# The last stage's quantizer hands three passes to ScalarE and its transposes wait one tile, and V is prepared two tiles to a bank

## The chip, the cores and the metric

One Trainium2 chip; the kernel runs on all eight of its cores. The metric is the device time of the slowest core, in microseconds. Each core has TensorE (PE, matmuls and their weight loads), VectorE (DVE), ScalarE (ACT), GpSimd (POOL, here only for issuing DMAs) and SyncE (SP, the same). No core waits for another.

## The reference

One transformer layer on x of shape (4, 4096, 1024): a layer norm, an attention over 8 heads of 256 whose keys and values come from a latent of 64, and, beside it on the same normed x, a feed-forward of width 2816 whose inputs and weights are quantized to FP4 and back.

```
xn = layernorm(x)
q = xn @ Wq.T;  kv = xn @ Wkv_down.T;  k = kv @ Wk_up.T;  v = kv @ Wv_up.T
attn = softmax(q k^T / 16) v @ Wo.T            # 8 heads
fq(t): per block of 16: scale = max(max|t| / 6, 1e-12); |t| / scale to the
       grid 0, .5, 1, 1.5, 2, 3, 4, 6; times sign(t) * scale
h = silu(fq(xn) @ fq(w_gate).T) * (fq(xn) @ fq(w_up).T)
out = x + attn + fq(h) @ fq(w_down).T
```

## The kernel before

Core c has half of one batch: 2048 tokens of its own, and the 4096 tokens of the batch as keys. Every engine's instruction list is written out by hand: `eb.em(engine, ...)` appends an instruction to that engine's queue, and `eb.wait(engine, sem, v)` appends a wait until a semaphore has reached v. An engine works its queue in order. Five stages follow one another with barriers between them.

1. Layer norm and quantization of x by DVE, transposes by PE (L340 to L393).
2. The latent and the queries (L435 to L483), and the bounds that take the place of a running maximum in the softmax.
3. Attention, head by head (L589 to L788). A head begins with its preparation. `emit_prep` makes the keys (indices 0 to 15, matmul L618, each 128x512 into one of four PSUM banks `PR4` = psA, psB, psE, psF in turn) and the values (indices 16 to 47, matmul L627, each 128 tokens x 256 into half of a bank). Results with an even index leave PSUM through ACT (L621, L630), those with an odd one through DVE (L623, L631). The values are made in eight groups of four. After each group ACT squares a part of the keys (L654, twice), PE sums the squares (L662) and DVE takes a maximum (L672, L676 or L678). PE's queue has the group's four value matmuls, then L662 twice, then the next group's. Then come the scores (L729), Exp (L743) and the product with V (L759) of four query blocks of 512. After each query block DVE has four units of weight quantization in its queue (`emit_wq_units`), each of which runs the quantizer over 128x512.
4. Softmax denominators and the output projection (L831 to L885).
5. The feed-forward (L927 to L1053). For each of two halves of the width (`ig`) the weights are loaded transposed (L934, L938, L942), and for each half of the tokens (`half`, 1024 each) there is a pass over eight tiles `tt` of 128 tokens. I call it a half pass; there are four. A tile has three chunks of 512, 512 and 384 columns: eight gate matmuls L958 into psD0 and eight up matmuls L962 into psD1, then Silu on ACT (L974) into `gs_c` and the product on DVE (L978) into `h_t`. Both banks are single, so the next chunk's matmuls wait for that product (`hbld`). Then the quantizer takes all 1408 columns of `h_t`, and its last instruction L238 writes `hq_t`. Eleven transposes in f32 (L994, three groups into psA and psB in turn) and three copies on ACT (L1005) bring it to `hqT_b` in bf16. After the eighth tile come the down-projections L1029, 176 matmuls, each of whose 16 results DVE adds to the residual (L1042).

The order in the queues of stage 5 is that of the code: PE has the transposes of a tile right behind its matmuls, ahead of the next tile's; DVE has three products and then the quantizer.

`emit_quant` is one routine for weights, x and h. With `F` columns, in order: L204 block maxima; L205 |t| into pA; L206 and L210 the sign (2 or 0, then 1 or -1) into pK; L208 and L212 the scale and its reciprocal, for F/16 blocks; L214 sign times scale; L217 |t| over scale; L219 to L230 the seven comparisons with the grid; L233 their sum; and L238 the result. The semaphore `lad` counts them, and `wt` waits for one of them.

Of the kernel before, what the change touches and what calls it, by code (L numbers as in the profile page):

```python
# [6 lines left out]
F32 = mybir.dt.float32  # L7
# [75 lines left out]
def build_program(debug=False, stop_after=9):  # L83
# [46 lines left out]
    S = {}  # L130
    for s in ["x_in", "lnv", "lna", "lnd", "lnap", "xq", "tr", "trev",
# [3 lines left out]
              "ffh", "sil", "hbld", "hq", "fftr", "fftrev", "ffdn", "ssq", "srw", "wkl", "lad"]:  # L135
# [45 lines left out]
    def emit_quant(eb, F, src, dst, PL):  # L181
# [3 lines left out]
        L = S['lad']  # L185

# [402 lines left out]
    for h in range(NH):  # L589
# [17 lines left out]
        def emit_prep(rng):  # L607
            for idx in rng:
# [38 lines left out]
        for grp in range(8):  # L647
            emit_prep(range(16 + 4 * grp, 16 + 4 * grp + 4))
# [264 lines left out]
    hq_t = sb("hq_t", [128, 1408], F32, es_b5)  # L913
# [12 lines left out]
    ftr_glob = 0  # L926
    for ig in range(2):  # L927
# [19 lines left out]
        for half in range(2):  # L947
            toff = half * 1024
            eb.wait('scalar', S['avq'], S['avq'].n)
            for tt in range(8):  # L950
                for ci, (c0, clen) in enumerate(NCH):
# [19 lines left out]
                    if S['hbld'].n > 0:  # L971
# [15 lines left out]
                for b_ in range(3):
                    js = [4, 4, 3][b_]
                    pbk = SBK[ftr_glob % 2]
                    if ftr_glob >= 2:  # L990
                        eb.wait('tensor', S['fftrev'], ftr_glob - 1)
                    for j in range(js):
                        c = b_ * 4 + j
                        ins = (lambda e, c=c, j=j, pbk=pbk: e.transpose(  # L994
                            pbk[:, j * 128:(j + 1) * 128], hq_t[:, c * 128:(c + 1) * 128], ident_t[:]))
                        if j == js - 1:
                            S['fftr'].n += 1
                            eb.em('tensor', lambda e, ins=ins: ins(e).then_inc(S['fftr'].h, 1))
                        else:
                            eb.em('tensor', ins)  # L1000
                    eb.wait('scalar', S['fftr'], S['fftr'].n)
                    S['fftrev'].n += 1
                    dst = hqT_b[:, b_ * 4:b_ * 4 + js, tt * 128:(tt + 1) * 128]
                    src = pbk[:, 0:js * 128].rearrange("p (c n) -> p c n", c=js)
# [97 lines left out]
```

## Time and profile before

| | us |
|---|---|
| median of 3 runs (4534.31 to 4548.57) | 4536.94 |
| the profiled execution, device time | 4542.34 |
| its span, first to last instruction of the slowest core | 4540.5 |
| spans of the eight cores | 4522.9 to 4540.5 |
| busy in the span: PE, DVE, ACT | 2552.1, 2607.8, 1116.9 |

The engines' busy times are sums over stages with different limits; the stages themselves are told apart by cutting the span into stretches. Times below are in microseconds from the span's start unless marked ns. The last stage's matmuls begin at 3008. The profile also gives the granted clock of TensorE: 1.00 is its level of 2.4 GHz, 0.50 that of 1.2 GHz.

### The profile page before, as it was taken

The page shows a single profiled execution, that of the slowest core. Times are in us where ns is not written, and L with a number is a line of the kernel's source. Part 1 is how long each engine was busy: PE and PEld are TensorE (multiplying, and loading weights), DVE is VectorE, ACT ScalarE, POOL GpSimd, SP SyncE. Part 2 cuts the span into 40 slices and gives each one's busy share as a digit, 9 for nine tenths or more (in the row PEclk, how much of TensorE's full clock was granted, in tenths as well). Part 3 has the DMA queues.
Part 4 walks back from the last instruction along what each step waited for, and adds up shares of the span by engine and source line. Part 5 has one row for each costly group of instructions (what it writes and reads, how often), then busy time and mean ns, then how long its engine had stood idle before and what let it go on. Part 6 is the DMA issues. An engine that isn't in the chain of part 4 may idle for free. (4 is left out here: it accounts for less than half of the span.)

```text
span 4540.5 us, 36505 instructions; the slowest of 8 cores (4522.9 to 4540.5 us)
## 1 busy us (share of the span) xinstructions
PE 2552.1 (56%) x9848; PEld 950.3 (21%) x9848; DVE 2607.8 (57%) x4169; ACT 1116.9 (25%) x1835; POOL 105.7 (2%) x199
## 2 busy tenths in 40 slices
PE   1113193197878787878888786823353352335335
PEld 1112040022222222222222222411121121112112
DVE  7888604757585857575757524125645542564554
ACT  1112030154545454545444450000000000000000
POOL 0000000000000000000000000000000000000000
PEclk9999995598888888898989795966787676668777
DMA  1112210001010101010101002350020015002002
GB/s 47 29 36 79 48 19 0 29 22 35 22 35 21 37 17 40 18 35 19 34 16 33 18 10 56 141 111 0 0 74 0 0 64 87 0 0 74 0 0 65
DMA packets 126530, 156.30 MB, mean 34 GB/s; under 512 B 77824, under 2 KB 88320, under 8 KB 124288
## 3 DMA queue, kind: packets, MB, share of 16 engines
q1 hardware_dynamic: 110368, 127.56, 10.1%
q0 software_dynamic: 15968, 26.42, 2.4%
q8 instruction: 89, 1.46, 0.1%
q14 instruction: 105, 0.86, 0.1%
HBM read 98.89 MB, written 46.66 MB: 32 GB/s over the span
## 5 line engine op out<-in xcount | busy, mean ns | idle before, releaser
L743 ACT ACTIVATE pbuf<-psA,negB_col 128x512 bf16<-128x512 f32 x512 | 352.1, 688 | 349.5 <-PE psA L729 349.5
L978 DVE TENSOR_TENSOR h_t<-gs_c,psD 128x512 f32<-128x512 f32 (+1 forms) x96 | 61.7, 643 | 650.4 <-ACT gs_c L974 650.4
L743 ACT ACTIVATE pbuf<-psB,negB_col 128x512 bf16<-128x512 f32 x512 | 351.4, 686 | 287.6 <-PE psB L729 286.9
L958 PE MATMUL psD<-wgq_b,xqT_sb 128*128 128x512 bf16 (+1 forms) x768 | 209.6, 426 | 232.5 <-DMA wdq_b<-WdqN 124.3
L204 DVE TENSOR_REDUCE pbm<-wbuf 128x32 f32<-128x512 f32 (+1 forms) x136 | 91.2, 670 | 401.1 <-DMA WdqN<-wqout 163.5
L759 PE MATMUL psC<-pbuf,V_h 128*128 128x512 bf16 x1024 | 310.9, 386 | 18.5 <-ACT pbuf L743 18.5
L759 PE MATMUL psD<-pbuf,V_h 128*128 128x512 bf16 x1024 | 304.5, 379 | 27.5 <-ACT pbuf L743 27.5
L729 PE MATMUL psA<-qT_all,kT_h 128*128 128x512 bf16 x1024 | 316.6, 392 | 0.4 <-DVEq L701 0.4
L729 PE MATMUL psB<-qT_all,kT_h 128*128 128x512 bf16 x1024 | 313.6, 388 | 0.0
L994 PE MATMUL psB<-ident_t,hq_t 128*128 128x128 f32 x176 | 48.3, 426 | 375.3 <-DVE hq_t L238 375.0
L994 PE MATMUL psA<-ident_t,hq_t 128*128 128x128 f32 x176 | 48.3, 425 | 375.2 <-DVE hq_t L238 375.2
L974 ACT ACTIVATE gs_c<-psD 128x512 f32<-128x512 f32 (+1 forms) x96 | 53.9, 562 | 656.8 <-PE psD L962 656.8
L759 PE MATMUL psE<-pbuf,V_h 128*1 128x512 bf16 x512 | 195.7, 382 | 0.0
L759 PE MATMUL psF<-pbuf,V_h 128*1 128x512 bf16 x512 | 193.0, 377 | 0.0
L962 PE MATMUL psD<-wuq_b,xqT_sb 128*128 128x512 bf16 (+1 forms) x768 | 168.6, 363 | 0.0
L1029 PE MATMUL psC<-hqT_b,wdq_b 128*128 128x512 bf16 x704 | 164.0, 397 | 4.9 <-ACT hqT_b L1005 3.3
L958 PEld LDWEIGHTS psD<-wgq_b,xqT_sb 128*128 128x128 bf16 x768 | 82.1, 112 | 349.7 <-issue 309.6
L326 PE MATMUL psA<-ident_t,xq_f 128*128 128x128 f32 x64 | 17.4, 427 | 232.5 <-DVE xq_f L238 232.5
L759 PEld LDWEIGHTS psC<-pbuf,V_h 128*128 128x128 bf16 x1024 | 98.4, 98 | 150.4 <-issue 39.7
L759 PEld LDWEIGHTS psD<-pbuf,V_h 128*128 128x128 bf16 x1024 | 97.6, 98 | 153.6 <-issue 40.8
L1042 DVE TENSOR_TENSOR obuf<-rbuf,psC 128x512 f32<-128x512 f32 x64 | 43.8, 688 | 140.8 <-PE psC L1029 118.4
L1005 ACT CAST hqT_b<-psB 128x512 bf16<-128x512 f32 (+1 forms) x48 | 26.4, 550 | 392.5 <-PE psB L994 392.5
(197 smaller groups left out, 4426.6 us busy)
## 6 DMA issues: line engine op xcount, KB each, us to landing
xbuf<-x_tok SPq DMA_DIRECT2D x16, 1024.0 KB, 6.0
rbuf<-resid_scr SPq DMA_DIRECT2D x32, 512.0 KB, 5.3
wbuf<-Wg SPq DMA_DIRECT2D x44, 256.0 KB, 2.8
wbuf<-Wu SPq DMA_DIRECT2D x44, 256.0 KB, 2.8
wbuf<-Wd SPq DMA_DIRECT2D x40, 256.0 KB, 2.7
xt_buf<-xT_own SPq DMA_DIRECT2D x8, 1024.0 KB, 6.8
resid_scr<-rstage SPq DMA_DIRECT2D x8, 1024.0 KB, 4.7
resid_scr<-obuf SPq DMA_DIRECT2D x16, 512.0 KB, 2.9
```

The lines of the kernel that those rows point to most:

```text
L204: t_bm = op(lambda e: e.tensor_reduce(out=pbm[:, 0:NB], in_=src3, axis=AX.X, op=ALU.max, apply_absolute_value=True))
L729: ins = (lambda e, h=h, qq=qq, kc=kc, m=m, pb=pb: e.matmul(pb[:, :], kT_h[:, m, kc * 128:(kc + 1) * 128], qT_all[:, 2 * h + m, qq * 512:(q ...
L743: eb.em('scalar', lambda e, cglob=cglob, pb=pb: e.activation(out=pbuf[:, cglob % 2, :], in_=pb[:, :], func=AF.Exp, bias=negB_col[:], scale ...
L759: ins = (lambda e, kc=kc, cg=cg, lo=lo, hi=hi, dstp=dstp, dsl=dsl: e.matmul(dstp[dsl, 0:512], V_h[:, kc, lo:hi], pbuf[:, cg % 2, :], start ...
L958: eb.em('tensor', lambda e, tt=tt, c0=c0, clen=clen, kc2=kc2, pg=pg, toff=toff: e.matmul(pg[:, 0:clen], xqT_sb[:, kc2, toff + tt * 128:tof ...
L962: ins = (lambda e, tt=tt, c0=c0, clen=clen, kc2=kc2, py=py, toff=toff: e.matmul(py[:, 0:clen], xqT_sb[:, kc2, toff + tt * 128:toff + (tt + ...
L974: eb.em('scalar', lambda e, clen=clen, pg=pg: e.activation(out=gs_c[:, 0:clen], in_=pg[:, 0:clen], func=AF.Silu).then_inc(S['sil'].h, 1))
L978: eb.em('vector', lambda e, c0=c0, clen=clen, py=py: e.tensor_tensor(out=h_t[:, c0:c0 + clen], in0=gs_c[:, 0:clen], in1=py[:, 0:clen], op= ...
L994: ins = (lambda e, c=c, j=j, pbk=pbk: e.transpose(pbk[:, j * 128:(j + 1) * 128], hq_t[:, c * 128:(c + 1) * 128], ident_t[:]))
L1005: eb.em('scalar', lambda e, dst=dst, src=src: e.copy(dst, src).then_inc(S['fftrev'].h, 1))
L1029: ins = (lambda e, m=m, n2=n2, it=it, pb=pb: e.matmul(pb[:, :], wdq_b[:, it, m * 128:(m + 1) * 128], hqT_b[:, it, n2 * 512:(n2 + 1) * 512] ...
L1042: eb.em('vector', lambda e, m=m, n2=n2, pb=pb: e.tensor_tensor(out=obuf[:, m % 2, n2 * 512:(n2 + 1) * 512], in0=rbuf[:, m % 2, n2 * 512:(n ...
```

## The change

It has three parts.

1. `emit_quant` gets an option `act_abs`, used in stage 5 alone. With it, ACT writes |t| into pA (Abs) and the sign into pK (Sign) and counts them in a new semaphore `aab`; L205, L206 and L210 are left out on DVE. ACT waits first for the quantizer of the tile before (`hq`) and for this tile's products (`hbld`). DVE waits for Sign ahead of L214 and for Abs ahead of L217. At the start of each tile DVE waits for `aab`.
2. `hq_t` has two buffers. The transposes of a tile and their copies are no longer put into the queues behind its quantizer, but behind the next tile's; those of the last tile of a half pass are put right behind.
3. In the preparation of a head the 32 value matmuls are taken in pairs. Two write the two halves of one bank, and one instruction of 128x512 takes both out. A group has two such pairs in place of four single matmuls: the first pair's bank is emptied by ACT, the second's by DVE.

The diff, cut to its core:

```
@@ -178,11 +178,19 @@
     SBK = [psA, psB]
     OAB = [(psC0, psC1, psE), (psD0, psD1, psF)]
 
-    def emit_quant(eb, F, src, dst, PL):
+    def emit_quant(eb, F, src, dst, PL, act_abs=False):
         NB = F // 16
         pA, pC, pD, pK = PL['pA'], PL['pC'], PL['pD'], PL['pK']
         v = 'vector'
         L = S['lad']
+        if act_abs:
+            AB = S['aab']
+            AB.n += 1
+            eb.em('scalar', lambda e: e.activation(out=pA[:, 0:F], in_=src, func=AF.Abs).then_inc(AB.h, 1))
+            a_abs = AB.n
+            AB.n += 1
+            eb.em('scalar', lambda e: e.activation(out=pK[:, 0:F], in_=src, func=AF.Sign).then_inc(AB.h, 1))
+            a_sg = AB.n
 
         def op(fn, inc=True):
             if inc:
@@ -202,18 +210,26 @@
         sb_ = pscale[:, 0:NB].unsqueeze(2).broadcast_to([128, NB, 16])
         rb = prcp[:, 0:NB].unsqueeze(2).broadcast_to([128, NB, 16])
         t_bm = op(lambda e: e.tensor_reduce(out=pbm[:, 0:NB], in_=src3, axis=AX.X, op=ALU.max, apply_absolute_value=True))
-        t_abs = op(lambda e: e.scalar_tensor_tensor(out=pA[:, 0:F], in0=src, scalar=-1.0, in1=src, op0=ALU.mult, op1=ALU.max))
-        t_sg = op(lambda e: e.tensor_scalar(out=pK[:, 0:F], in0=src, scalar1=0.0, scalar2=2.0, op0=ALU.is_ge, op1=ALU.mult))
+        if not act_abs:
+            t_abs = op(lambda e: e.scalar_tensor_tensor(out=pA[:, 0:F], in0=src, scalar=-1.0, in1=src, op0=ALU.mult, op1=ALU.max))
+            t_sg = op(lambda e: e.tensor_scalar(out=pK[:, 0:F], in0=src, scalar1=0.0, scalar2=2.0, op0=ALU.is_ge, op1=ALU.mult))
         wt(t_bm)
         t_sc = op(lambda e: e.tensor_scalar(out=pscale[:, 0:NB], in0=pbm[:, 0:NB], scalar1=6e-12, scalar2=1.0 / 6.0, op0=ALU.max, op1=ALU.mult))
-        wt(t_sg)
-        t_sg1 = op(lambda e: e.tensor_single_scalar(out=pK[:, 0:F], in_=pK[:, 0:F], scalar=1.0, op=ALU.subtract))
+        if not act_abs:
+            wt(t_sg)
+            t_sg1 = op(lambda e: e.tensor_single_scalar(out=pK[:, 0:F], in_=pK[:, 0:F], scalar=1.0, op=ALU.subtract))
         wt(t_sc)
         t_rcp = op(lambda e: e.reciprocal(prcp[:, 0:NB], pscale[:, 0:NB]))
-        wt(t_sg1)
+        if act_abs:
+            eb.wait(v, S['aab'], a_sg)
+        else:
+            wt(t_sg1)
         t_ss = op(lambda e: e.tensor_tensor(out=K3, in0=K3, in1=sb_, op=ALU.mult))
         wt(t_rcp)
-        wt(t_abs)
+        if act_abs:
+            eb.wait(v, S['aab'], a_abs)
+        else:
+            wt(t_abs)
         t_A = op(lambda e: e.tensor_tensor(out=A3, in0=A3, in1=rb, op=ALU.mult))
         wt(t_A)
         tc = op(lambda e: e.tensor_single_scalar(out=pC[:, 0:F], in_=pA[:, 0:F], scalar=0.25, op=ALU.is_gt))
@@ -615,22 +631,28 @@
                         eb.wait('tensor', S['qpj'], kv_base_d + pidx // 2 + 1)
...
                 else:
-                    mt = idx - 16
-                    ins = (lambda e, h=h, mt=mt, pb=pb: e.matmul(
+                    mt = (idx - 16) * 2
+                    ins2 = [(lambda e, h=h, mt=mt, pb=pb: e.matmul(
                         pb[0:128, 0:256], kvT_b[:, mt * 128:(mt + 1) * 128],
-                        wvuh[:, h % 2, :], start=True, stop=True))
-                    eva = (lambda e, mt=mt, pb=pb: e.copy(V_h[:, mt, 0:256], pb[0:128, 0:256]))
-                    evd = (lambda e, mt=mt, pb=pb: e.tensor_copy(V_h[:, mt, 0:256], pb[0:128, 0:256]))
-                S['prep'].n += 1
-                eb.em('tensor', lambda e, ins=ins: ins(e).then_inc(S['prep'].h, 1))
+                        wvuh[:, h % 2, :], start=True, stop=True)),
+                            (lambda e, h=h, mt=mt, pb=pb: e.matmul(
+                        pb[0:128, 256:512], kvT_b[:, (mt + 1) * 128:(mt + 2) * 128],
+                        wvuh[:, h % 2, :], start=True, stop=True))]
+                    dst = V_h[:, mt:mt + 2, 0:256]
+                    srcp = pb[0:128, 0:512].rearrange("p (c n) -> p c n", c=2)
+                    eva = (lambda e, dst=dst, srcp=srcp: e.copy(dst, srcp))
+                    evd = (lambda e, dst=dst, srcp=srcp: e.tensor_copy(dst, srcp))
+                for k2, ins in enumerate(ins2):
+                    S['prep'].n += 1
+                    eb.em('tensor', lambda e, ins=ins: ins(e).then_inc(S['prep'].h, 1))
                 if idx % 2 == 0:
                     eb.wait('scalar', S['prep'], S['prep'].n)
                     S['kvev'].n += 1
@@ -645,7 +667,7 @@
         eb.wait('scalar', S['qpj'], kv_base_d + 8)
         mmp_tgt = [0] * 8
         for grp in range(8):
-            emit_prep(range(16 + 4 * grp, 16 + 4 * grp + 4))
+            emit_prep(range(16 + 2 * grp, 16 + 2 * grp + 2))
             if grp >= 1:
                 eb.wait('scalar', S['bnd'], mmp_tgt[grp - 1])
             sq_base = S['sco'].n
@@ -910,7 +932,7 @@
     wdq_b = sb("wdq_b", [128, 11, 1024], BF16, es_b5)
     gs_c = sb("gs_c", [128, 512], F32, es_b5)
     h_t = sb("h_t", [128, 1408], F32, es_b5)
-    hq_t = sb("hq_t", [128, 1408], F32, es_b5)
+    hq_t = sb("hq_t", [128, 2, 1408], F32, es_b5)
     hqT_b = sb("hqT_b", [128, 11, 1024], BF16, es_b5)
     rbuf = sb("rbuf", [128, 2, 1024], F32, es_b5)
     obuf = sb("obuf", [128, 2, 1024], F32, es_b5)
@@ -924,6 +946,32 @@
     IG = [0, 1408]
     NCH = [(0, 512), (512, 512), (1024, 384)]
     ftr_glob = 0
+    lgq = 0
+    pend_tr = None
+
+    def emit_tr(eb, lg, tt, hq_tgt):
+        nonlocal ftr_glob
+        eb.wait('tensor', S['hq'], hq_tgt)
+        for b_ in range(3):
+            js = [4, 4, 3][b_]
+            pbk = SBK[ftr_glob % 2]
+            if ftr_glob >= 2:
+                eb.wait('tensor', S['fftrev'], ftr_glob - 1)
+            for j in range(js):
+                c = b_ * 4 + j
+                ins = (lambda e, c=c, j=j, pbk=pbk, lg=lg: e.transpose(
+                    pbk[:, j * 128:(j + 1) * 128], hq_t[:, lg % 2, c * 128:(c + 1) * 128], ident_t[:]))
+                if j == js - 1:
+                    S['fftr'].n += 1
+                    eb.em('tensor', lambda e, ins=ins: ins(e).then_inc(S['fftr'].h, 1))
+                else:
+                    eb.em('tensor', ins)
+            eb.wait('scalar', S['fftr'], S['fftr'].n)
+            S['fftrev'].n += 1
+            dst = hqT_b[:, b_ * 4:b_ * 4 + js, tt * 128:(tt + 1) * 128]
+            src = pbk[:, 0:js * 128].rearrange("p (c n) -> p c n", c=js)
+            eb.em('scalar', lambda e, dst=dst, src=src: e.copy(dst, src).then_inc(S['fftrev'].h, 1))
+            ftr_glob += 1
     for ig in range(2):
         i0 = IG[ig]
         if True:
@@ -948,6 +996,7 @@
             toff = half * 1024
             eb.wait('scalar', S['avq'], S['avq'].n)
             for tt in range(8):
+                eb.wait('vector', S['aab'], S['aab'].n)
                 for ci, (c0, clen) in enumerate(NCH):
                     s_ = half * 24 + tt * 3 + ci
                     pg = psD0
@@ -978,32 +1027,22 @@
                     eb.em('vector', lambda e, c0=c0, clen=clen, py=py: e.tensor_tensor(
                         out=h_t[:, c0:c0 + clen], in0=gs_c[:, 0:clen], in1=py[:, 0:clen],
                         op=ALU.mult).then_inc(S['hbld'].h, 1))
+                lg = lgq
+                eb.wait('scalar', S['hq'], S['hq'].n)
+                eb.wait('scalar', S['hbld'], S['hbld'].n)
                 eb.wait('vector', S['hbld'], S['hbld'].n)
-                eb.wait('vector', S['fftr'], S['fftr'].n)
-                last = emit_quant(eb, 1408, h_t[:, 0:1408], hq_t[:, 0:1408], PL5)
+                if lg >= 2:
+                    eb.wait('vector', S['fftr'], 3 * (lg - 1))
+                last = emit_quant(eb, 1408, h_t[:, 0:1408], hq_t[:, lg % 2, 0:1408], PL5, act_abs=True)
                 S['hq'].n += 1
                 eb.em('vector', lambda e, last=last: last(e).then_inc(S['hq'].h, 1))
-                eb.wait('tensor', S['hq'], S['hq'].n)
...
+                if pend_tr is not None:
+                    pend_tr()
+                pend_tr = (lambda lg=lg, tt=tt, hq_tgt=S['hq'].n: emit_tr(eb, lg, tt, hq_tgt))
+                lgq += 1
+            if pend_tr is not None:
+                pend_tr()
+                pend_tr = None
             if debug and half == 0 and ig == 0:
                 eb.wait('sync', S['fftrev'], S['fftrev'].n)
                 S['out'].n += 16
```

## Rows read from the trace of the kernel before

**Rows 1.** The page's costliest groups: busy, mean ns, idle ahead and its releaser.

```profile
L994 PE MATMUL psB<-ident_t,hq_t 128*128 128x128 f32 x176 | 48.3, 426 | 375.3 <-DVE hq_t L238 375.0
```

**Rows 2.** Engines by stretch: PE, PEld, DVE, ACT, POOL busy, clock; first half pass, sum.

```profile
3008.00:3337.00 329.00, 113.78 (x472) 56.58 (x472) 185.00 (x160) 26.69 (x48) 0.00 (x0) 0.70 0.01 3
...
sum 1307.00, PE 445.75 PEld 223.95 DVE 741.38 ACT 105.88 POOL 0.00; mean PE 111.44 PEld 55.99 DVE 185.34 ACT 26.47 POOL 0.00
```

**Rows 3.** The timeline of one tile in the middle of a half pass.

```profile
3260.23 0.69 DVE L978 TENSOR_TENSOR h_t<-gs_c,psD 128x512 f32<-128x512 f32 x1 [8.91 <-ACT gs_c L974]
...
3261.06 1.89 PE L958 MATMUL psD<-wgq_b,xqT_sb 128*128 128x512 bf16 x8 [1.68 <-DVE h_t L978]
...
3266.36 1.46 PE L958 MATMUL psD<-wgq_b,xqT_sb 128*128 128x384 bf16 x8 [1.69 <-DVE h_t L978]
...
3270.63 1.62 DVE L204 TENSOR_REDUCE pbm<-h_t 128x88 f32<-128x1408 f32 x1 [0.21 <-DVE h_t L978]
...
3274.51 0.20 DVE L208 TENSOR_SCALAR pscale<-pbm 128x88 f32<-128x88 f32 x1
...
3275.50 0.70 DVE L212 RECIPROCAL prcp<-pscale 128x88 f32<-128x88 f32 x1
3276.12 1.56 DVE L214 TENSOR_TENSOR PL5pK<-PL5pK,pscale 128x1408 f32<-128x1408 f32 x1
...
3290.66 1.63 DVE L238 TENSOR_TENSOR hq_t<-PL5pC,PL5pK 128x1408 f32<-128x1408 f32 x1 [0.17 <-DVE PL5pC L233]
```

**Rows 4.** The timeline around the first down-projection and the second half pass.

```profile
3331.62 1.63 DVE L238 TENSOR_TENSOR hq_t<-PL5pC,PL5pK 128x1408 f32<-128x1408 f32 x1 [0.17 <-DVE PL5pC L233]
...
3337.11 40.91 PE L1029 MATMUL psC<-hqT_b,wdq_b 128*128 128x512 bf16 x176 [0.82 <-ACT hqT_b L1005]
...
3377.86 1.89 PE L958 MATMUL psD<-wgq_b,xqT_sb 128*128 128x512 bf16 x8
...
3392.73 1.62 DVE L204 TENSOR_REDUCE pbm<-h_t 128x88 f32<-128x1408 f32 x1 [0.21 <-DVE h_t L978]
```

**Rows 5.** ACT's groups by form, last stage and squares of the keys.

```profile
L654 ACT ACTIVATE sqv_t<-kT_h 128x512 bf16<-128x512 bf16 x128 | 73.7, 627 | 0.0
L974 ACT ACTIVATE gs_c<-psD 128x512 f32<-128x512 f32 x64 | 38.2, 597 | 533.6 <-PE psD L962 533.6
...
L974 ACT ACTIVATE gs_c<-psD 128x384 f32<-128x384 f32 x32 | 15.7, 491 | 123.2 <-PE psD L962 123.2
...
L920 ACT ACT_TABLE_LOAD x1 | 1.3, 1283 | 229.4 <-PEq L892 229.4
```

**Rows 6.** The chain that ended last, at starts of chunk 0.

```profile
3008.41 3.47 PE psD L958 x8
3011.88 1.74 PE psD L962 x8
...
3254.36 3.29 PE psD L958 x8
...
3798.64 3.57 PE psD L958 x8
3802.21 2.46 PE psD L962 x8
```

**Rows 7.** DVE's groups by form, one line of the quantizer.

```profile
L222 DVE SCALAR_TENSOR_TENSOR PL3pC<-PL3pA,PL3pC 128x512 f32<-128x512 f32 x112 | 76.8, 685 | 0.0
...
L222 DVE SCALAR_TENSOR_TENSOR PL2pC<-PL2pA,PL2pC 128x512 f32<-128x512 f32 x8 | 5.5, 686 | 0.0
```

**Rows 8.** The timeline of one group of V's preparation.

```profile
898.65 0.39 PE L627 MATMUL psA<-wvuh,kvT_b 64*128 64x256 bf16 x1
...
898.84 0.42 PE L627 MATMUL psB<-wvuh,kvT_b 64*128 64x256 bf16 x1
...
899.14 0.37 ACT L630 CAST V_h<-psA 128x256 bf16<-128x256 f32 x1 [1.57 <-PE psA L627]
...
899.83 1.15 ACT L654 ACTIVATE sqv_t<-kT_h 128x512 bf16<-128x512 bf16 x2
```

More of the change, by code:

```diff
@@ L134, in build_program @@
               "xt16", "rs", "rr", "out", "fw", "xqr", "kv_pe", "q_pe", "prep", "pbev",
-              "ffh", "sil", "hbld", "hq", "fftr", "fftrev", "ffdn", "ssq", "srw", "wkl", "lad"]:
+              "ffh", "sil", "hbld", "hq", "fftr", "fftrev", "ffdn", "ssq", "srw", "wkl", "lad", "aab"]:
         S[s] = Sem(nc, es_sh, "s_" + s)
@@ L617, in emit_prep @@
                     m, n = idx // 8, idx % 8
-                    ins = (lambda e, h=h, m=m, n=n, pb=pb: e.matmul(
+                    ins2 = [(lambda e, h=h, m=m, n=n, pb=pb: e.matmul(
                         pb[:, :], wkuh[:, h % 2, m * 128:(m + 1) * 128],
-                        kvT_b[:, n * 512:(n + 1) * 512], start=True, stop=True))
+                        kvT_b[:, n * 512:(n + 1) * 512], start=True, stop=True))]
                     eva = (lambda e, m=m, n=n, pb=pb: e.copy(
@@ L980, in build_program @@
                         op=ALU.mult).then_inc(S['hbld'].h, 1))
+                lg = lgq
+                eb.wait('scalar', S['hq'], S['hq'].n)
+                eb.wait('scalar', S['hbld'], S['hbld'].n)
                 eb.wait('vector', S['hbld'], S['hbld'].n)
-                eb.wait('vector', S['fftr'], S['fftr'].n)
-                last = emit_quant(eb, 1408, h_t[:, 0:1408], hq_t[:, 0:1408], PL5)
+                if lg >= 2:
+                    eb.wait('vector', S['fftr'], 3 * (lg - 1))
+                last = emit_quant(eb, 1408, h_t[:, 0:1408], hq_t[:, lg % 2, 0:1408], PL5, act_abs=True)
                 S['hq'].n += 1
                 eb.em('vector', lambda e, last=last: last(e).then_inc(S['hq'].h, 1))
-                eb.wait('tensor', S['hq'], S['hq'].n)
[L987 to L1004, printed above, removed]
-                    eb.em('scalar', lambda e, dst=dst, src=src: e.copy(dst, src).then_inc(S['fftrev'].h, 1))
-                    ftr_glob += 1
+                if pend_tr is not None:
[5 more added lines that the diff above has]
+                pend_tr = None
             if debug and half == 0 and ig == 0:
```

## The prediction

> **What bounds the kernel now.** I read the page's costliest groups first. The transposes of `hq_t` idle 375 us behind the last instruction of the quantizer, twice, once for each bank [rows 1]: in the last stage TensorE waits for VectorE, tile after tile. Then I cut the last stage into stretches. Its four half passes over eight token tiles, from the first gate matmul to the first down-projection matmul, take 1307 us of the 4540.5, and in them PE is busy 446 us and DVE 741 us, with a granted clock of 0.70 [rows 2]. Neither engine is full: they take turns. The timeline of one tile says how [rows 3]. Chunk 1 starts at 3261.06, chunk 2 at 3266.36, the quantizer's first instruction L204 at 3270.63, and its last, L238, ends at 3290.66 + 1.63 = 3292.29. That is 21.66 us; transposes and chunk 0 of the next tile follow only then, which is PE's idleness of [rows 1]. One tile takes about 1307 / 32 = 40.8 us.
>
> The attention stage has another limit, and the change touches it at one place, the preparation of V, read from the timeline of one group [rows 8].
>
> **Part 1: three DVE passes go to ACT.** L205, L206 and L210 leave the quantizer of the last stage. What is left ahead of L214: L204 (1.62 us), L208 (0.20), L212 (0.70, but it starts 0.62 ahead of L214) [rows 3]. A result that is waited for costs 0.17 more, as ahead of L238 [rows 3]; before, other instructions covered this. So L208 starts 1.62 + 0.17 = 1.79 us after L204, L212 at 1.79 + 0.20 + 0.17 = 2.16, L214 at 2.78, where it started at 3276.12 - 3270.63 = 5.49. The quantizer falls by 2.71 to 18.95 us, if Abs and Sign are ready.
>
> No row has Abs or Sign. ACT took 597 ns for 512 columns and 491 for 384, 0.83 ns a column; 128x512 from SBUF took 627 [rows 5]. For 1408 columns that is 0.627 + 896 x 0.00083 = 1.37 us. Both may start when the last h_t product is done, 0.1 us ahead of L204, as their other wait is for the quantizer before. The second follows 0.1 early as ACT's do, and ends at -0.1 + 1.27 + 1.37 = 2.54, with 0.1 for the wait 2.64: just in time for L214 at 2.78. Bounds: L214 can't come before L204 allows, so the gain is at most 2.71; if ACT ran these at twice my price, L214 would be 2.6 later and the gain would be nothing. I take 2.71, because ACT's rows agree on the rate. The Trainium skill ("ScalarE: Activation LUTs", Rules for kernel authors) speaks against this move: simple elementwise work such as max and mul belongs on VectorE, with up to 3x in bf16. Here the data are f32 and the passes leave the engine that everybody waits for. By the rule the move would gain nothing, and the sum would be that of the rival "ACT is slow" below; no row of this case times the two functions.
>
> **Part 2: transposes one tile late.** `emit_tr` of tile t-1 now stands behind the matmuls of tile t, so in PE's queue the order is chunks 0 to 2 of tile t, transposes of t-1, chunk 0 of t+1. All of the last two can run under quantizer t. Chunk 1 can't: its banks psD0/psD1 are single, so it waits for the product L978 of chunk 0, which DVE does behind quantizer t. So the serial chain of a tile becomes
>
> - quantizer: 18.95
> - from its end to chunk 1: L978 starts 0.1 early (nothing awaited), takes 0.69, and PE follows 0.14 later (3260.23 + 0.69 to 3261.06 [rows 3]): 0.73
> - chunk 1 to chunk 2: 5.30; chunk 2 to L204: 4.27 [rows 3]
>
> Together 29.25 us, at the full clock. But PE now idles between chunk 0 and chunk 1. What lies under the quantizer: transposes, of which the third group must wait for the first group's copy, which on ACT stands behind Abs and Sign (2.5 + 0.6 + 0.1 = 3.2 us after L204), three more transposes with at most 3 x 0.43 = 1.3 [rows 1], and chunk 0 with at most 16 x 0.43 = 6.9, ends by 11.4, with its Silu at about 12. Chunk 1 comes at 18.95 + 0.73 = 19.7. So the cover has 7 to 8 us to spare, and PE pays that idleness with its clock. Rows: after the idle times ahead of the first and third half pass, the first eight matmuls took 3.47 and 3.57 us in place of 1.74, and in the third half pass the next eight took 2.46 [rows 6]: 0.43 us a matmul is the 1.2 GHz level, 0.22 the 2.4 GHz one. The loss is 1.73 and 1.83 + 0.72 = 2.55 us. Before, this loss fell on chunk 0; now on chunk 1. A tile in the middle of a pass lost 3.29 - 1.74 = 1.55 [rows 6], with transposes ahead of its chunk 0. I take 1.7, between the two lower ones, since most tiles are such. A tile then takes 29.25 + 1.7 = 30.95 us; with the bounds 1.55 and 2.55 it is 30.8 to 31.8, and with all 16 matmuls at the low level (3.4) 32.65.
>
> The second `hq_t` buffer serves only this delay: L238 waits for transposes two tiles back, long done. The new wait of DVE for ACT at each tile's head asks for what L214 has already had. Nothing new goes to SP, POOL or a DMA queue in this stage.
>
> **A half pass.** The first tile has nothing to overlap: 3392.73 - 3377.86 = 14.87 us from chunk 0 to L204 [rows 4], plus the clock's 1.73 and 2.55 in the first and third pass. Then seven periods, a last quantizer of 18.95, and from its end to the down-projection 3337.11 - (3331.62 + 1.63) = 3.86 [rows 4], as the last transposes have no cover. All four: 4 x (14.87 + 18.95 + 3.86) + 4.3 + 28 x 30.95 = 150.7 + 4.3 + 866.6 = 1021.6 us. Before 1307: the change is -285 us. The down-projections read and write the same and stay.
>
> **Part 3: V two tiles to a bank.** The 256 V matmuls stay; 256 evictions of 256 columns become 128 of 512, shared as before between ACT and DVE. What sets a group's length is the start of Square L654, for which PE's next matmuls wait; DVE's evictions lie beside it. Before, it starts 899.83 - 898.65 = 1.18 after the first V matmul. After, ACT waits for the second matmul, like the one that ends at 898.84 + 0.42 = +0.61; plus 0.10 it starts the copy, whose 512 columns let Square start 0.60 - 0.10 = 0.50 later [rows 5, 8]: 1.21. That is 0.03 a group, 64 groups, +2 us; I call it nothing. Bounds: the whole of one saved eviction (0.37 x 64 = -24 us), and a second matmul wholly exposed (0.42 x 64 = +27). The price follows the rows closely, so I keep 10 us of them each way.
>
> **Sum.** 4542.3 (profiled execution) - 285 = 4257; against its span, 4540.5 - 285 = 4255. The profiled execution was 5 us above the median of 4536.9, which gives 4536.9 - 285 = 4252 us. Its own range is 4228 to 4285.
>
> **Rivals.**
>
> - *A table load for Sign.* If Sign is not in the table that holds Silu, ACT loads on the way to Sign and back to Silu. A load took 1.28 us [rows 5]; the first delays L214, the second is under the quantizer. 32 x (2.64 + 1.28 - 2.78) = 36 us: 4288. Against it: Square, Exp and copies alternate in the attention stage with no load but the stages' three. The Trainium skill (same page, Table sets: the hidden batching unit) lists copy, identity, relu and abs as in every set, and does not list sign. No run yet shows it. Chance 0.04.
> - *ACT is slow.* At twice my price for Abs and Sign, L214 waits for ACT, 32 x 2.6 = 83 us: 4335. Against it ACT's rate in [rows 5]. Chance 0.03.
> - *The clock stays low.* Chunks 1 and 2 entirely at 1.2 GHz: 3.4 + 2.6 in place of 1.7, 28 x 4.3 = 120 us: 4372. For it: more but shorter idle times. Against it: it rose in each pass while chunk 0 ran [rows 6]. Chance 0.05.
> - *No overlap of chunk 0.* If its Silu came behind something that lasts as long as the quantizer, a tile had some 5.0 + 1.7 us more: 28 x 6.7 = 188 us, 4440. Against it the 7 to 8 us to spare. Chance 0.04.
> - *Slower: contention under the quantizer.* Before, DVE quantized alone; now PE and ACT use the memories meanwhile. If this stretched DVE's instructions, each per cent would cost 32 x 0.19 = 6 us. From 285 / 6 = 47% on, the kernel is slower; at 60% it takes 4252 + 364 = 4616. Against it: the same L222 took 685 ns while attention ran on PE and ACT, and 686 with DVE alone [rows 7]. Chance 0.01.
>
> **How the numbers follow.** Forecast 0.83, rivals 0.17 together. The range of 8 in 10 takes the V part's 10 us and an excess of the clock to 2.55, and reaches to the table load: 4225 to 4292. A measurement of this kernel can tell a change of about 0.3%, 14 us, from none; every case but the last is far beyond it on the faster side. Faster 0.97, same 0.01, slower 0.02 (contention, and something unnamed).
>
> **What would show it.** Right: L205, L206 and L210 absent from the last stage's DVE, L204 to the end of L238 18.95 us, two ACT instructions of 1.37; PE's transposes and a chunk of 16 matmuls under it; chunk 1 with matmuls of 0.43 first; tiles 31 us apart; half passes of 252 to 256 us; Square 1.2 us behind a group's first V matmul, as before. Wrong: ACT_TABLE_LOAD more than three times; DVE's L214 waiting for ACT; chunk 2 at 0.33 us a matmul; L978 waiting for its Silu right behind the quantizer.

## The result, and the profile after

The changed kernel takes 0.9376 of the time of the kernel before, 95% interval 0.9353 to 0.9399. On the 4541 us that the kernel before took in these runs that is 4258 us, 283 us less (273 to 294). The forecast was 4252. The profiled execution took 4249.6 us, its span 4248.0.

Numbers in what follows that combine a run's ratio with a time use the same 4541 us. A few executions in which the cores of one die ran at a lower clock are left out of all ratios. Line numbers moved: L204 is L212 now, L208 L217, L212 L222, L214 L227, L238 L254; the transposes L994 are L962 and their copies L973, the matmuls L958 and L962 are L1007 and L1011, Silu is L1023, the product L1027 and the down-projection L1068.

The last stage first, the four half passes as stretches (busy time of PE, PEld, DVE, ACT, POOL, then the granted clock, as in [rows 2]):

```profile
3006.00:3262.00 256.00, 118.94 (x472) 55.03 (x472) 160.51 (x136) 46.32 (x64) 0.00 (x0) 0.74 0.01 4
...
sum 1028.00, PE 478.85 PEld 220.55 DVE 643.19 ACT 184.83 POOL 0.00; mean PE 119.71 PEld 55.14 DVE 160.80 ACT 46.21 POOL 0.00
```

These stretches are cut at whole microseconds, and the last, from 3950 to 4207, reaches 2.7 us into the down-projection, which starts at 4204.29. From the first gate matmul to the first down-projection matmul the four passes take 256.1, 257.1, 258.0 and 253.7 us, together 1025, where they took 1307. PE has the same matmuls and 30 us more of busy time, as more of them run at the low clock; DVE has 98 us less, which is the three passes that left it; ACT 79 us more. A tile in the middle of the first half pass answers to [rows 3]:

```profile
3177.90 1.38 ACT L189 ACTIVATE PL5pA<-h_t 128x1408 f32<-128x1408 f32 x1 [0.75 <-DVE h_t L1027]
3178.02 1.62 DVE L212 TENSOR_REDUCE pbm<-h_t 128x88 f32<-128x1408 f32 x1 [0.21 <-DVE h_t L1027]
3179.18 1.36 ACT L192 ACTIVATE PL5pK<-h_t 128x1408 f32<-128x1408 f32 x1
...
3180.45 0.56 ACT L973 CAST hqT_b<-psA 128x512 bf16<-128x512 f32 x1
3180.68 1.60 DVE L227 TENSOR_TENSOR PL5pK<-PL5pK,pscale 128x1408 f32<-128x1408 f32 x1
...
3181.83 3.62 PE L1007 MATMUL psD<-wgq_b,xqT_sb 128*128 128x512 bf16 x8
...
3188.24 0.60 ACT L1023 ACTIVATE gs_c<-psD 128x512 f32<-128x512 f32 x1 [5.63 <-PE psD L1011]
...
3195.25 1.63 DVE L254 TENSOR_TENSOR hq_t<-PL5pC,PL5pK 128x1408 f32<-128x1408 f32 x1 [0.17 <-DVE PL5pC L249]
...
3197.62 3.45 PE L1007 MATMUL psD<-wgq_b,xqT_sb 128*128 128x512 bf16 x8 [9.54 <-DVE h_t L1027]
...
3208.76 1.62 DVE L212 TENSOR_REDUCE pbm<-h_t 128x88 f32<-128x1408 f32 x1 [0.21 <-DVE h_t L1027]
```

Count from L212 at 3178.02. Abs starts 0.12 ahead of it, Sign 1.28 later, and Sign ends at 3180.54. L227 needs it and starts at 3180.68, 2.66 after L212, with no idle time of its own: ACT is just in time. The quantizer ends at 3196.88, after 18.86 us. Under it PE has the last transposes, held until ACT's first copy at 3180.45 + 0.56, and chunk 0, whose Silu starts at 3188.24. Then PE idles until 3197.62. Chunk 1 begins there with eight matmuls in 3.45 us, the low clock: TensorE's granted clock had fallen during this idle time, and from 3192 to 3200 it was 0.50. The next tile's quantizer starts at 3208.76: 30.74 us from tile to tile.

The chain that ended last shows how a pass settles (starts and lengths; L1007 x8 is the first half of a chunk, L1011 x8 the second):

```profile
3042.25 3.57 PE psD L1007 x8
3045.82 2.49 PE psD L1011 x8
...
3074.22 3.57 PE psD L1007 x8
...
3105.22 3.57 PE psD L1007 x8
...
3197.62 3.45 PE psD L1007 x8
...
3262.20 39.84 PE psC L1068 x176
...
3336.36 3.57 PE psD L1007 x8
3339.93 2.22 PE psD L1011 x8
3344.10 2.68 PE psD L1007 x8
3346.77 1.78 PE psD L1011 x8
...
4204.29 39.85 PE psC L1068 x176
```

Chunk 1 of the pass's second tile needs 3.57 + 2.49 us where the high clock would give 3.48, a loss of 2.6. The next ones begin 31.97 and 31.00 us later and lose 2.0 and 1.83, until at 3197.62 the loss is 1.7; from there the tiles are 30.73 apart. The other passes settle in the same way, but from other values: the second tile of the second pass (3336.36) loses 2.3 us in chunk 1 and 1.7 more in chunk 2, where the granted clock was low again, and takes 33.3 us in all. PE idled 16.1 us ahead of chunk 1 in that tile, as in the second tile of the first and the third pass, and 9.5 us in the settled tile above. The first down-projection takes 39.84 us where it took 40.91 [rows 4].

ACT's groups, beside [rows 5]:

```profile
L189 ACT ACTIVATE PL5pA<-h_t 128x1408 f32<-128x1408 f32 x32 | 44.1, 1377 | 24.4 <-DVE h_t L1027 24.4
L192 ACT ACTIVATE PL5pK<-h_t 128x1408 f32<-128x1408 f32 x32 | 43.5, 1360 | 0.0
...
L942 ACT ACT_TABLE_LOAD x1 | 1.3, 1283 | 230.6 <-PEq L914 230.6
```

Abs and Sign took 1.38 and 1.36 us. The table load is one of the same three as before, so Abs and Sign run between two Silus without a load of their own.

And one group of V's preparation, beside [rows 8]: two matmuls fill psA, one ACT copy takes both out, and Square follows.

```profile
897.31 0.39 PE L643 MATMUL psA<-wvuh,kvT_b 64*128 64x256 bf16 x1
...
897.50 0.42 PE L646 MATMUL psA<-wvuh,kvT_b 64*128 64x256 bf16 x1
...
898.01 0.59 ACT L651 CAST V_h<-psA 128x512 bf16<-128x512 f32 x1 [1.78 <-PE psA L646]
...
898.49 1.15 ACT L676 ACTIVATE sqv_t<-kT_h 128x512 bf16<-128x512 bf16 x2
```

Square starts 898.49 - 897.31 = 1.18 us after the group's first matmul. Before it was 1.18.

### The profile page after: what moved, and what is told of

It reads as the page before. It is cut to its first block and busy times, and to the rows that moved or that the text cites. A ratio compares the mean times of both kernels' runs of the same rounds, so it can differ in the third digit from the quotient of the medians.

```text
span 4248.0 us, 36150 instructions; the slowest of 8 cores (4236.9 to 4248.0 us)
## 1 busy us (share of the span) xinstructions
PE 2576.2 (61%) x9848; PEld 946.0 (22%) x9848; DVE 2505.2 (59%) x4009; ACT 1185.5 (28%) x1835; POOL 106.1 (2%) x199
## 5 line engine op out<-in xcount | busy, mean ns | idle before, releaser
L1007 PE MATMUL psD<-wgq_b,xqT_sb 128*128 128x512 bf16 (+1 forms) x768 | 251.7, 491 | 502.3 <-DVE h_t L1027 379.6
L1027 DVE TENSOR_TENSOR h_t<-gs_c,psD 128x512 f32<-128x512 f32 (+1 forms) x96 | 61.6, 641 | 458.5 <-ACT gs_c L1023 458.5
L212 DVE TENSOR_REDUCE pbm<-wbuf 128x32 f32<-128x512 f32 (+1 forms) x136 | 91.2, 670 | 400.8 <-DMA WdqN<-wqout 163.0
L1023 ACT ACTIVATE gs_c<-psD 128x512 f32<-128x512 f32 (+1 forms) x96 | 53.9, 562 | 967.4 <-PE psD L1011 967.4
L781 PE MATMUL psC<-pbuf,V_h 128*128 128x512 bf16 x1024 | 311.0, 386 | 17.9 <-ACT pbuf L765 17.8
L1007 PEld LDWEIGHTS psD<-wgq_b,xqT_sb 128*128 128x128 bf16 x768 | 89.2, 122 | 644.1 <-issue 621.7
L1011 PE MATMUL psD<-wuq_b,xqT_sb 128*128 128x512 bf16 (+1 forms) x768 | 186.8, 390 | 0.0
L1068 PE MATMUL psC<-hqT_b,wdq_b 128*128 128x512 bf16 x704 | 159.4, 391 | 3.3 <-ACT hqT_b L973 3.3
L781 PEld LDWEIGHTS psD<-pbuf,V_h 128*128 128x128 bf16 x1024 | 97.5, 97 | 153.6 <-issue 40.8
L342 PE MATMUL psA<-ident_t,xn_scr 128*128 128x128 f32 x128 | 34.8, 427 | 134.4 <-DVE xn_scr L385 134.4
L888 PE MATMUL psC<-o_all,wo_b 128*128 128x512 bf16 x512 | 112.9, 384 | 1.5 <-DVE o_all L870 1.5
L1011 PEld LDWEIGHTS psD<-wuq_b,xqT_sb 128*128 128x128 bf16 x768 | 82.9, 108 | 103.3 <-issue 47.6
```

Of the source, the lines that this page charges most:

```text
L212: t_bm = op(lambda e: e.tensor_reduce(out=pbm[:, 0:NB], in_=src3, axis=AX.X, op=ALU.max, apply_absolute_value=True))
L342: ins = (lambda e, c=c, j=j, pbank=pbank, src_tile=src_tile: e.transpose(pbank[:, j * 128:(j + 1) * 128], src_tile[:, c * 128:(c + 1) * 12 ...
L781: ins = (lambda e, kc=kc, cg=cg, lo=lo, hi=hi, dstp=dstp, dsl=dsl: e.matmul(dstp[dsl, 0:512], V_h[:, kc, lo:hi], pbuf[:, cg % 2, :], start ...
L888: ins = (lambda e, m=m, n=n, kc=kc, pb=pb: e.matmul(pb[:, :], wo_b[:, kc, m * 128:(m + 1) * 128], o_all[:, kc, n * 512:(n + 1) * 512], sta ...
L1007: eb.em('tensor', lambda e, tt=tt, c0=c0, clen=clen, kc2=kc2, pg=pg, toff=toff: e.matmul(pg[:, 0:clen], xqT_sb[:, kc2, toff + tt * 128:tof ...
L1011: ins = (lambda e, tt=tt, c0=c0, clen=clen, kc2=kc2, py=py, toff=toff: e.matmul(py[:, 0:clen], xqT_sb[:, kc2, toff + tt * 128:toff + (tt + ...
```

## The experiments

**The parts one by one.** Each is the kernel before with one part of the change. `e_act` has part 1: the transposes are put behind each quantizer again (`hq_t` keeps its two buffers, which then serve nothing).

```diff
-                if pend_tr is not None:
-                    pend_tr()
-                pend_tr = (lambda lg=lg, tt=tt, hq_tgt=S['hq'].n: emit_tr(...))
+                emit_tr(eb, lg, tt, S['hq'].n)
```

> Part 1 alone: Abs and Sign on ACT, but the transposes right behind each tile's quantizer and V as before. Theory A (costs add): each of 32 quantizers is 2.7 to 2.8 us shorter and the matmuls' loss to the low clock stays at about 1.55 us, so tiles are 38.2 us apart in place of 40.96 and the kernel takes 4541 - 32 x 2.75 = 4453 us. Theory B (the loss depends on how the idle time falls, and settles with the period): the loss moves by up to 1 us a tile, tiles are 37.2 to 39.2 apart and equal once settled, 4425 to 4485 us. Theory C (ACT's copies and waits are what counts, not DVE): no change, 4541.

Ratio 0.9763 (0.9732 to 0.9793), 4433 us. The chain, at the starts of chunk 0:

```profile
3196.92 2.88 PE psD L1001 x8
...
3234.67 2.78 PE psD L1001 x8
...
3272.33 2.72 PE psD L1001 x8
```

Tiles are 37.75 and 37.66 us apart, not 38.2. The quantizer is 18.86 us as in the changed kernel, so DVE's 2.8 us are as priced; but chunk 0 loses only 2.88 - 1.74 = 1.14, then 1.04 and 0.98 us to the low clock, where it lost 1.55 [rows 6]. Theory A has the gain some 20 us too small, theory B holds, theory C falls. Of those 20 us the clock is one part: the 28 tiles of the trace are 86 us shorter in sum, and 28 x 2.8 = 78 of them are the quantizer's.

`e_late` has part 2 alone:

```diff
-                last = emit_quant(eb, 1408, ..., PL5, act_abs=True)
+                last = emit_quant(eb, 1408, ..., PL5)
```

> Part 2 alone: transposes one tile late with two buffers, quantizer all on DVE as before, V as before. Theory A (a fixed loss of 1.7 us to the low clock): the tile takes 21.66 + 0.73 + 5.30 + 4.27 + 1.7 = 33.65 us against 40.96, 28 x 7.3 = 205 us less, 4336 us. Theory B (the loss settles with the period): the changed kernel's chunk 1 lost 1.7 us in settled tiles and up to 2.9 in the first ones, so settled tiles here lie between 33.5 and 34.9 us apart, each with the same value, 4336 to 4375 us. Rival (the gain of the change is in the shorter quantizer): 4480 or more.

Ratio 0.957 (0.9545 to 0.9596), 4346 us. The chain, at the starts of chunk 1:

```profile
3500.87 3.57 PE psD L1001 x8
3504.44 2.00 PE psD L1005 x8
...
3534.77 3.57 PE psD L1001 x8
3538.34 2.12 PE psD L1005 x8
...
3569.15 3.57 PE psD L1001 x8
```

Tiles are 33.90 and 34.38 us apart, and a chunk loses (3.57 - 1.74) + (2.00 - 1.74) = 2.09 and then 2.21 us, more than the 1.7 of the changed kernel. There are two pairs to compare. In the kernel before and in `e_act` the transposes run first after the idle time, at the low clock, and chunk 0 behind them loses 1.55 and 0.98 us; PE had idled some 23 and 21 us. In the changed kernel and here chunk 1 comes first and loses 1.7 and 2.2 us; PE had idled 9.5 and 17.8 us. In both pairs the loss changed with the quantizer's length, so it is no constant that can be carried from one kernel to another. Whether the length of the idle time sets it or the period of the tiles was not tried apart. By its time alone this run agrees with theory A too (4336 lies in its interval); the tiles, 33.9 to 34.4 apart and not 33.65, are what speaks for theory B. The rival that the shorter quantizer is most of the gain falls: part 2 is.

`e_v` has part 3 alone, `e_noV` is the change without it. They differ in `emit_prep` as in the diff above.

> Part 3 alone: V two tiles to a bank, last stage as before. My working gives +0.03 us a group, 64 groups, +2 us: 4543. The rival that an eviction less is time saved gives up to -24 us: 4517; the rival that the second matmul of a pair is exposed gives up to +27: 4568.

Ratio 0.9976 (0.9949 to 1.0003): 4530 us, with no change inside the interval. One group:

```profile
895.57 0.39 PE L627 MATMUL psE<-wvuh,kvT_b 64*128 64x256 bf16 x1
...
896.75 1.15 ACT L660 ACTIVATE sqv_t<-kT_h 128x512 bf16<-128x512 bf16 x2
...
898.99 0.39 PE L627 MATMUL psA<-wvuh,kvT_b 64*128 64x256 bf16 x1
```

Square comes at +1.18, and the next group's first matmul 3.42 us after this one's, as in the kernel before (898.65 and 902.07 there). Both rivals would need some 0.4 us a group and are out.

> The change without its part 3 (V as before). With the V part alone a head's values took 24.97 in place of 25.06 us, so theory: the same as the changed kernel, 4258 plus or minus 3 us. Rival (part 3 gave the 0.24% that its own run had below the kernel before): 11 us more, 4269.

Ratio 0.9365 (0.934 to 0.939), 4253 us; with part 3 it was 0.9376 (0.9353 to 0.9399). Part 3 does nothing that these runs can tell. In per cent of the kernel before, parts 1 and 2 alone give 2.4 and 4.3, together 6.7; both at once give 6.35. Each interval is 0.25 to 0.3 wide to either side, so the two agree; what the tiles show is plainer. From the 40.97 us of a settled tile, part 1 takes 3.4, part 2 some 6.8, both 10.2.

**The low clock of chunk 1.** Added matmuls stand in PE's queue ahead of chunk 1's wait and write a bank that nobody reads. `pop` takes the wait out of the queue, and it is put back behind them; the second of the two runs has 46 in place of 36:

```diff
+                    if ci == 1 and tt > 0:
+                        eb.q['tensor'].pop()
+                        for f_ in range(36):
+                            eb.em('tensor', lambda e, f_=f_: e.matmul(
+                                psE[:, 0:512], xqT_sb[:, f_ % 8, 0:128],
+                                wgq_b[:, f_ % 8, 0:512], start=True, stop=True))
+                        eb.wait('tensor', S['hbld'], hb_base + s_)
```

> The changed kernel with 36 matmuls of 512 columns more in each tile but a pass's first, between chunk 0 and chunk 1, into a bank that nobody reads: 7.8 us at the high clock, under the quantizer. Theory (chunk 1 pays for PE's idleness with the low clock): chunk 1 then runs in 3.5 in place of 5.2 us, tiles are 29.1 us apart, 28 x 1.7 to 2.2 = 48 to 60 us less than the changed kernel, about 4200 us. Rival (the first matmuls of chunk 1 are slow for another reason, such as the wait for DVE): no change, 4258. Rival (the added matmuls reach beyond the quantizer): slower, 4270 or more.

Ratio 0.9351 (0.9315 to 0.9387), 4246 us, not apart from the changed kernel. About 4200 was expected: a miss, and the timeline says why:

```profile
3803.20 7.93 PE L1009 MATMUL psE<-wgq_b,xqT_sb 128*128 128x512 bf16 x36
...
3814.20 3.04 PE L1014 MATMUL psD<-wgq_b,xqT_sb 128*128 128x512 bf16 x8 [3.06 <-DVE h_t L1034]
```

The 36 matmuls end at 3811.13 and PE idles 3.06 us ahead of chunk 1, whose first eight matmuls take 3.04 us instead of 1.89. The granted clock was still 1.00 in that idle time, 0.79 in the first microsecond of chunk 1 and 0.50 in the next three: it fell just after PE had begun again. So the test didn't take enough of the idleness away, and most tiles took 30.86 us. In the same execution two tiles came out otherwise. One is this:

```profile
3224.45 1.89 PE L1014 MATMUL psD<-wgq_b,xqT_sb 128*128 128x512 bf16 x7 [1.75 <-DVE h_t L1034]
```

Here chunk 0 had been slower, the added matmuls ended later and PE idled only 1.75 us. Chunk 1 ran at the high clock, and the tile took 29.18 us. The next run shortens the idle time in all tiles:

> As the run with 36 added matmuls a tile, but 46: 9.9 us at the high clock. There PE still idled 3.06 us ahead of chunk 1, the clock was low again when chunk 1 began or fell in it, and tiles were 30.86 us apart. Theory (it is the idleness that costs chunk 1 its clock): with about 1 us of idleness left, chunk 1 takes 3.5 us and tiles are 29.2 us apart, 28 x 1.6 = 45 us less than the changed kernel, 4213. Rival (the loss is not from idleness): 4255 as before. Rival (added matmuls overrun in tiles where they start late at the low clock): 4230 to 4260.

```profile
3793.34 1.89 PE L1014 MATMUL psD<-wgq_b,xqT_sb 128*128 128x512 bf16 x8 [2.56 <-DVE h_t L1034]
...
3802.91 1.62 DVE L212 TENSOR_REDUCE pbm<-h_t 128x88 f32<-128x1408 f32 x1 [0.21 <-DVE h_t L1034]
...
3811.42 10.09 PE L1009 MATMUL psE<-wgq_b,xqT_sb 128*128 128x512 bf16 x46
...
3832.09 1.62 DVE L212 TENSOR_REDUCE pbm<-h_t 128x88 f32<-128x1408 f32 x1 [0.21 <-DVE h_t L1034]
```

Ratio 0.9281 (0.9268 to 0.9294), 4215 us, 43 below the changed kernel. Chunk 1 at 3793.34 runs at 0.22 us a matmul throughout, though PE idled 2.56 us ahead of it. In other tiles of this run that idle time is anything from nothing to 2.9 us. A settled tile takes 29.18 us (3832.09 - 3802.91), most of them 29.17; I had worked out 29.25 at the full clock. The loss of the changed kernel's settled tiles, 30.73 - 29.17 = 1.56 us, is the price of PE's idleness, and 46 matmuls without use are cheaper than none: 28 x 1.56 = 44 us.

**What holds a tile at 30.7.** Three pairs of banks and three parts of `gs_c`, one for each chunk:

```diff
-                    pg = psD0
-                    py = psD1
-                    if s_ >= 1:
-                        eb.wait('tensor', S['hbld'], hb_base + s_)
+                    pg, py = [(psD0, psD1), (psE, psF), (psC0, psC1)][ci]
+                    if s_ >= 3:
+                        eb.wait('tensor', S['hbld'], hb_base + s_ - 2)
+                    if tt == 0 and ci == 2:
+                        eb.wait('tensor', S['ffdn'], S['ffdn'].n)
...
-                        eb.wait('scalar', S['hbld'], S['hbld'].n)
+                    eb.wait('scalar', S['hbld'], S['hbld'].n - 2)
...
-    gs_c = sb("gs_c", [128, 512], F32, es_b5)
+    gs_c = sb("gs_c", [128, 3, 512], F32, es_b5)
```

> The changed kernel with a pair of PSUM banks and a third of gs_c for each of the three chunks, so that all matmuls and Silus of a tile can run under the quantizer of the one before. Theory (the single pair of banks holds chunks 1 and 2 and their Silus on the serial chain of a tile): DVE alone bounds a tile, 18.9 for the quantizer and about 2.1 for three products and the handover, 21.0 us in place of 30.8, and each pass's first tile is 2 us shorter: 4258 - 28 x 9.8 - 8 = 3975 us. Rival (PE at the low clock becomes the bound: transposes held up to 6 us by ACT, then 16 to 17 us of matmuls): tiles of 23 us, 4040. Rival (another wait holds the chunks): 4258.

> The kernel with three pairs of banks once more, since its first measurement had too few comparable runs for an interval. If it is bound as its trace shows (tiles 20.73 us apart, 28.5 to 30 us of the three-bank gain a pass), 3948 us, a ratio to the kernel before of 0.869; anything above 0.89 would say that the first profile was not typical.

The first measurement gave no interval; its profiled execution had a span of 3949.6 us. The second gave a ratio of 0.8702 (0.8675 to 0.8729), 3952 us, 306 below the changed kernel. The timeline of a tile, from the first of the two:

```profile
3101.28 1.62 DVE L212 TENSOR_REDUCE pbm<-h_t 128x88 f32<-128x1408 f32 x1 [0.21 <-DVE h_t L1027]
...
3105.09 3.20 PE L1008 MATMUL psD<-wgq_b,xqT_sb 128*128 128x512 bf16 x8
...
3109.85 1.89 PE L1008 MATMUL psE<-wgq_b,xqT_sb 128*128 128x512 bf16 x8
...
3116.22 0.49 ACT L1023 ACTIVATE gs_c<-psC 128x384 f32<-128x384 f32 x1 [2.00 <-PE psC L1012]
...
3118.51 1.63 DVE L254 TENSOR_TENSOR hq_t<-PL5pC,PL5pK 128x1408 f32<-128x1408 f32 x1 [0.17 <-DVE PL5pC L249]
3120.06 0.68 DVE L1027 TENSOR_TENSOR h_t<-gs_c,psD 128x512 f32<-128x512 f32 x1
...
3121.25 0.55 DVE L1027 TENSOR_TENSOR h_t<-gs_c,psC 128x384 f32<-128x384 f32 x1
...
3122.01 1.62 DVE L212 TENSOR_REDUCE pbm<-h_t 128x88 f32<-128x1408 f32 x1 [0.21 <-DVE h_t L1027]
```

All three chunks lie under the quantizer: the last Silu starts at 3116.22, 2.3 us ahead of the quantizer's last instruction. Then DVE has three products in a row and the next quantizer 3122.01 - 3101.28 = 20.73 us after the last. DVE has no idle time left but its short waits. Chunk 0 has its low clock here too (3.20 us for eight matmuls, which take 1.89 in chunk 1), at no cost. Both rivals fall. The theory's 3975 us was 23 too high: the tiles came at 20.73, not 21.0, and those of the changed kernel took 31.1 on average, not 30.8, which is some 15 of the 23. Banks and parts of `gs_c` were given together, so this run doesn't tell which of the two held the chunks, or whether both did.

`e_bank_dve` is that kernel with the three passes back on DVE (the edit of `e_late`):

> As the run with three pairs of banks, but the quantizer all on DVE. If DVE alone bounds a tile, its three passes cost their full 2.8 us in each tile, 32 x 2.8 = 90 us more than that run: about 4065. If PE bounds it, they cost less, down to nothing.

Ratio 0.8911 (0.8894 to 0.8929), 4046 us: 94 us more than with the passes on ACT, give or take 15 by the two intervals, where 32 x 2.8 = 90 was expected. The trace is sharper: its tiles are 23.52 us apart instead of 20.73, so the three passes cost 2.79 us a tile. With DVE as the bound they cost their full time, as worked out.

**How much slack ACT has.**

```diff
+            AB.n += 1
+            eb.em('scalar', lambda e: e.activation(out=pC[:, 0:F], in_=src, func=AF.Abs).then_inc(AB.h, 1))
             AB.n += 1
             eb.em('scalar', lambda e: e.activation(out=pA[:, 0:F], in_=src, func=AF.Abs).then_inc(AB.h, 1))
```

> The changed kernel with one more Abs of 128x1408 on ACT ahead of the two, into a tile that is overwritten later: Abs and Sign come 1.28 us later. In the changed kernel Sign ends 0.14 us ahead of the instruction that needs it, so that one is 1.2 us later and each quantizer takes 20.05. Theory A (costs add): 28 tiles and 4 last quantizers, 32 x 1.2 = 38 us more than the changed kernel, 4296. Theory B (the clock's loss settles with the period): between 15 and 60 us more. Rival (ACT has slack): 4258.

```profile
3396.03 1.62 DVE L214 TENSOR_REDUCE pbm<-h_t 128x88 f32<-128x1408 f32 x1 [0.21 <-DVE h_t L1029]
...
3399.92 1.63 DVE L229 TENSOR_TENSOR PL5pK<-PL5pK,pscale 128x1408 f32<-128x1408 f32 x1 [1.15 <-ACT PL5pK L194]
```

Ratio 0.9483 (0.9467 to 0.9498), 4306 us, 48 above the changed kernel. L229 (L214 in the kernel before) now idles 1.15 us for Sign and starts 3.89 us after L214, the quantizer's start here, 1.23 later than in the changed kernel. 32 x 1.23 = 39 us are as theory A has them. Of the other 9, the trace gives some 5 to the clock: its 28 tiles are 40.7 us longer in sum, where 28 longer quantizers (20.12 for 18.86) make 35. The rest is within the interval. The rival that ACT has slack falls: the 0.1 us is all there is.

## Why the prediction was right

- *The quantizer.* 18.95 us forecast, 18.86 measured; L214's successor at 2.66 after the start (2.78). Abs and Sign took 1.38 and 1.36 us where 1.37 was extrapolated from 512 and 384 columns. The two rivals on ACT, a table load and double durations, have no rows: three loads as before. `e_2abs` shows what a Sign that comes 1.2 us too late costs. The Trainium skill's rule for such work ("ScalarE: Activation LUTs", Rules for kernel authors) would have had the passes stay on VectorE. Taken as a rule for the time, it did not hold here: in f32 Abs on ACT takes 1.38 us where DVE's L205 took 1.62, Sign 1.36 where L206 and L210 took 0.89 each, `e_act` gained 2.4%, and `e_bank_dve` prices their absence from DVE at 2.8 us a tile.
- *The overlap.* Transposes and chunk 0 under the quantizer, chunk 1 held by its banks: shown by the timeline, and by `e_bank`, where chunk 1 is no longer held.
- *The serial chain.* 29.25 us at the full clock; `e_warm46` measured 29.17, and the quantizer's 0.09 is about the difference.
- *The clock.* The term was 1.7 us a tile, and it measured 1.9: the 28 tiles take 31.09 us on average, of which 29.17 are the serial chain. Two errors lie in it. The prediction counted the loss from 1.74 us for eight matmuls, but its 5.30 from chunk 1 to chunk 2 holds them at 1.89 already, as they are after a wait [rows 3], so 0.15 us a tile is counted twice, and a settled tile loses 1.56 in these terms. Against that, the first tiles of a pass lose far more, up to 4.0 us in the second pass. Together the passes take 1025.0 us where 1021.6 was forecast: 4.0 more in the 28 tiles, 0.6 less around them. The reason given for 1.7, that a settled tile before lost 1.55, was weak: the kernel before itself lost only 0.25 us in the second tile of its second pass (eight matmuls in 1.99 at 3417.42), `e_act` has the same order and lost 1.0, and `e_late`, with the order of the changed kernel, 2.2. That 1.7 came out near is luck.
- *What was called unchanged.* The down-projections gained about 1 us each (39.84 for 40.91, 39.85 for 40.81). This is the clock as well: from 3 to 6 us after the start of the first one it was 0.54 before and is 0.89 now. These 4 us about outweigh the 3.4 above.
- *V.* +2 us forecast, nothing found, and Square at the same 1.18.
- *Contention.* The slower rival has no row: DVE's L246 and L254 keep 1.62 and 1.63 us while PE and ACT work.

The measured 4258 us (4247 to 4268) can't be told from the forecast of 4252. The spans of the two profiled executions differ by 292.5 us, more than the 283 of the ratio: 282.2 in the passes, 6.3 in the down-projections, 2.4 in a last stage that starts earlier and 1.6 in the loading of weights between the halves. Of the 6.3, some 2.3 are not the clock's: on the core profiled before, three results of the last two down-projections waited for a transfer of `rbuf` of 7.5 to 8.0 us, and on two other cores of that execution the last one took 40.8 us with no such wait. That forecast and measurement lie this close owes something to small errors of opposite sign.

## What to carry to other kernels

When an engine waits for another tile after tile, write down the serial chain of a tile with its waits, and ask for each piece which buffer keeps it there. Here the delay of the transposes took off the chain the 8.9 us in which DVE waited for chunk 0 [rows 3], of which 6.8 were gained, as the low clock then fell on chunk 1; a second and third pair of banks with their parts of `gs_c` would have taken off another 10. Price a move from DVE to ACT by ACT's per-column rate, and check that the last result is there before it is needed: here 0.1 us was the whole margin. And treat the matmuls' clock after idleness as a range, not as a constant: here from 0.25 to 4.0 us a tile.

## What the runs showed of the hardware that was not expected

- What a tile lost to the low clock changed from kernel to kernel. In settled tiles chunk 0 behind the transposes lost 1.55 us before and 1.0 in `e_act`; chunk 1 right behind the idle time lost 1.7 in the changed kernel and 2.2 in `e_late`. Along a pass the loss drifted to one value (2.6, 2.0, 1.8, 1.7 in the changed kernel's first pass, from 4.0 down in its second; in the kernel before it rose in the second pass, from 0.25). In `e_2abs` it did not: by turns tiles took about 31.9 and 33.0 us. What sets these values was not tried.
- In `e_warm` PE idled 3.06 us ahead of a chunk, and the clock fell only once PE worked again: granted 1.00 in the idle time, 0.79 and then 0.50 in the chunk. In another tile of it PE idled 1.75 us, in one of `e_warm46` 2.56, and the clock stayed high throughout. In the changed kernel's settled tiles it fell during the idle time of 9.5 us.
- Ten microseconds of matmuls that nobody reads, in each of 28 tiles, made the kernel 43 us faster.
